# Expert layers: counting matmuls and the write of the gates moved into the next step

## The chip, the cores and the metric

One core of one Trainium2 chip runs the whole program. The metric is the time of one execution on the device, in microseconds. The engines are TensorE (PE; its weight loads are PEld), VectorE (DVE), ScalarE (ACT), GpSimd (POOL) and SyncE (SP), which issues the transfers.

## What is computed

The input x has 16 sequences of 512 tokens with 128 features. A mixture of experts, an attention with 16 heads, and the same mixture of experts again are each added to x. The change is in the expert layer, which runs twice:

```python
C = int(Tt * K / Ee * CAPACITY_FACTOR) + 1
logits = jnp.einsum('btd,ed->bte', x, Wr)
top_vals, top_idx = jax.lax.top_k(logits, K)
w = jax.nn.softmax(top_vals, axis=-1)
flat_e = top_idx.reshape(Bb, Tt * K)
oh = jax.nn.one_hot(flat_e, Ee, dtype=jnp.int32)
pos_all = jnp.cumsum(oh, axis=1) - oh
pos = jnp.take_along_axis(pos_all, flat_e[..., None], axis=-1)[..., 0]
keep = pos < C
...
expert_out = jnp.einsum('becd,edf->becf', expert_in, We)
...
out = jnp.einsum('btk,btkd->btd', w, gathered)

x = x + 0.5 * _L0_ffn_ref(_layernorm(x, axis=-1), L0_ffn_Wr, L0_ffn_We)
x = x + _L0_attn_ref(_layernorm(x, axis=-1), ...)
x = x + 0.5 * _L0_ffn_ref(_layernorm(x, axis=-1), L0_ffn_Wr, L0_ffn_We)
```

There are 8 experts, each token picks 2, and an expert takes only its first 193 picks of a sequence.

## The kernel before

x lies on chip the whole time, as 16 sequences of 4 tiles of 128 tokens. The expert layer computes all 8 experts for every token and weighs the products with gates, which are zero for experts that were not picked or were full. One step of the layer works on sequence b, while the routing of b + 1 and the statistics of b + 2 run between. Each engine has its own program; they wait for one another's semaphores, and each engine runs its instructions in the order written. The step is a function per engine (`step`, lines 313 to 330 for TensorE, 569 to 595 for VectorE).

TensorE, per step: it transposes the normalised sequence b + 1 (`turn_h`, L277), multiplies the first tile of b with four experts (`experts_lo`, the low product, L303) and with the other four (`experts_hi`, the high product, L310), multiplies b + 1 with the router (`logits`, L286), does the low and high products of tiles 1 to 3, and at the end counts, for every token of b + 1, the earlier picks of each expert (`places`, four bf16 matmuls, L293 and L295). Logits and counts lie in the two halves of one PSUM bank; the logits of b + 1 wait until all twelve parts of b's routing are done, the write of b's gates among them, the counts for the picks (7 parts).

VectorE, per step: statistics of b + 2 (L476, four instructions), then for each tile four additions to x of gate times low product (L561): two of this tile, two of the tile before. Between the additions stand the aggregates of the statistics (L483), eps (L490), the shift (L495, which waits for POOL's root L419), and the nine pieces of the routing of b + 1 (`route`): 0 the copy of the logits (L509), 1 the two largest, 2 their indices and gap, 3 the compares (L526, L528), 4 the picks (L532), 5 to 7 the weights (L536 to L545, with an exponential of ScalarE), and 8 the gates (L553): weight times (count below 193). `ROUTE_AFTER` says behind which addition (tile, number) a piece stands; piece 8 is last, behind the last addition of the step.

ScalarE copies the transposes, scales the four high products of a tile with the gates (L374) and normalises b + 2. POOL sums the scaled products (L426, L433), adds them to x (L440), and takes the root.

In either layer steps (counted from 0, like the sequences) run as straight code at the ends and as a loop of two steps in the middle (first layer: steps 1 to 8; second layer: 1 to 12). Steps 9 to 15 of the first layer have pieces of the attention between the tiles, and the second layer's first sequence is prepared inside the end of the attention (`late`). The last two steps of a layer have no statistics, the last no routing.

Of the kernel before, what the change touches and what calls it, by code (L numbers as in the profile page):

```python
# [57 lines left out]
def after(b, n):  # L58


    return not isinstance(b, int) or b > n
# [96 lines left out]
def expert_layer(nc, ctx, tag, x, consts, weights, banks, guard, x_in=None, out=None):  # L158
# [67 lines left out]
    def added(b, t, e):  # L226


        n = b * T + t
        if isinstance(n, int) and n == 0 and e < 2:  # L230
            return e + 1
        if isinstance(n, int) and n == NSEQ * T - 1 and e >= 2:
            return n * HE + e + 1
        return n * HE + (-1, 1, 4, 6)[e]
# [35 lines left out]
    def tensor_part():  # L270
        def turn_h(b, par):
            guard.turn_h(b)
            pe.wait_ge(hn_done, b + 1)
            if after(b, 0):
                pe.wait_ge(hT_copied, b)
            for t in range(T):
                mm = nc.tensor.transpose(hT_ps[:, t * P:(t + 1) * P], hn[:, t, :], consts.ident)  # L277
            mm.then_inc(hT_out, 1)

        def logits(b, par):  # L280
            guard.logits(b)
            pe.wait_ge(hT_copied, b + 1)
            if after(b, 0):
                pe.wait_ge(route_step, b * RT)
            for t in range(T):
                mm = nc.tensor.matmul(route_ps[:, 0, t, :], hT[par][:, t * P:(t + 1) * P], wrT[:],  # L286
                                      start=True, stop=True)
            mm.then_inc(logits_out, 1)

        def places(b):  # L290

            pe.wait_ge(route_step, b * RT + PICKED)
            nc.tensor.matmul(route_ps[:, 1, :, :], consts.before_b, picks[:], start=True, stop=False)  # L293
            for s in range(1, T):
                mm = nc.tensor.matmul(route_ps[:, 1, s:T, :], consts.ones_b, picks[:, 0:T - s, :],  # L295
                                      start=False, stop=(s == T - 1))
            mm.then_inc(places_out, 1)

        def experts_lo(b, par, t):
            guard.experts_lo(b, t)  # L300
            if after(b, 0):
                pe.wait_ge(acc_step, added(b - 1, t, HE - 1))
            nc.tensor.matmul(lo_ps[t][:], hT[par][:, t * P:(t + 1) * P], we[:, 0:HE, :],  # L303
                             start=True, stop=True).then_inc(lo_out, 1)

        def experts_hi(b, par, t):
            guard.experts_hi(b, t)
            if after(b, 0) or t >= 2:
                pe.wait_ge(scaled_done, b * T + t - 1)
            nc.tensor.matmul(hi_ps[t % 2][:], hT[par][:, t * P:(t + 1) * P], we[:, HE:E, :],  # L310
                             start=True, stop=True).then_inc(hi_out, 1)

        def step(b, par, half, this, next1, next2, between=None):
            if next1:
                turn_h(b + 1, 1 - par)
            if this:
                experts_lo(b, par, 0)
                if between:
                    between(0)
                experts_hi(b, par, 0)  # L320
            if next1:
                logits(b + 1, 1 - par)
            if this:
                for t in range(1, T):
                    if between:
                        between(t)
                    experts_lo(b, par, t)
                    experts_hi(b, par, t)
            if next1:
                places(b + 1)  # L330

        def begin():
            pe.wait_ge(consts.placed, consts.N_PLACED)
            pe.wait_ge(weights.placed, weights.N_PLACED)

        def late(what):
            if what == "turn_h":
                turn_h(0, 0)
            elif what == "logits":
                logits(0, 0)  # L340
            elif what == "places":
                places(0)

        return Part(begin, step, None, late)

    def scalar_part():
# [121 lines left out]
    def vector_part():  # L468
        def statistics(b, par, half):
            if x_in is not None:  # L470
                dve.wait_ge(x_loaded[par], half * DMA + DMA)
            guard.statistics(b)
            if after(b, 0):
                dve.wait_ge(nmr_done, b)
            for t in range(T):
                ins = nc.vector.bn_stats(bn[:, t, :], xt(b, t))  # L476
            ins.then_inc(bn_done, 1)

        def aggregate(b):
            dve.wait_ge(bn_done, b + 1)  # L480
            dve.sem_inc(dve_passed, 1)
            for t in range(T):
                ins = nc.vector.bn_aggr(mean_var[:, t, :], bn[:, t, :])  # L483
            ins.then_inc(stats_done, 1)

        def add_eps(b):
            dve.wait_ge(stats_done, b + 1)
            if after(b, 0):
                dve.wait_ge(rstd_done, b)
            nc.vector.tensor_scalar(veps[:], mean_var[:, :, 1], EPS, 0.0, ALU.add, ALU.add).then_inc(eps_added, 1)  # L490

        def shift_mean(b):

            dve.wait_ge(rstd_done, b + 1)
            nc.vector.scalar_tensor_tensor(out=nmr[:], in0=mean_var[:, :, 0], scalar=-1.0, in1=rstd[:],  # L495
                                           op0=ALU.mult, op1=ALU.mult).then_inc(nmr_done, 1)
# [60 lines left out]
        def add_expert(b, par, t, e):  # L557

            if e > 0:
                dve.wait_ge(acc_step, added(b, t, e - 1))  # L560
            nc.vector.scalar_tensor_tensor(out=xt(b, t), in0=lo_ps[t][:, e, :],  # L561
                                           scalar=gates[par][:, t, e:e + 1], in1=xt(b, t),
                                           op0=ALU.mult, op1=ALU.add).then_inc(acc_step, 1)


        ROUTE_AFTER = {(1, 0): [0], (1, 1): [1], (1, 2): [2], (1, 3): [3], (2, 0): [4], (2, 2): [5],
                       (2, 3): [6], (3, 0): [7], (3, 3): [8]}

        def step(b, par, half, this, next1, next2, between=None):
            if next2:  # L570
                statistics(b + 2, par, half)
            for t in range(T):
                if between:
                    between(t)
                if this:
                    dve.wait_ge(lo_out, b * T + t + 1)
                    if t == 0:
                        dve.wait_ge(route_step, b * RT + RT)
                        dve.wait_ge(hn_done, b + 1)
                for k in range(HE):  # L580
                    if this and k % 2 == 0:
                        add_expert(b, par, t, k // 2)
                    elif this and t > 0:
                        add_expert(b, par, t - 1, 2 + k // 2)
                    elif this and after(b, 0):
                        add_expert(b - 1, 1 - par, T - 1, 2 + k // 2)
                    if next1:
                        for n in ROUTE_AFTER.get((t, k), []):
                            route(b + 1, 1 - par, n)
                    if next2 and (t, k) == (0, 0):  # L590
                        aggregate(b + 2)
                    if next2 and (t, k) == (0, 1):
                        add_eps(b + 2)
                    if next2 and (t, k) == (1, 0):
                        shift_mean(b + 2)
# [23 lines left out]
        def late(what):  # L619
            if what in ("statistics0", "statistics1"):  # L620
                b = int(what[-1])
                statistics(b, b, 0)
                aggregate(b)
                add_eps(b)
            elif what in ("normalise0", "normalise1"):
                shift_mean(int(what[-1]))
                normalise(int(what[-1]))
            elif what == "turn_h":
                dve.wait_ge(hT_out, 1)
                nc.vector.tensor_copy(hT[0][:], hT_ps[:]).then_inc(hT_copied, 1)  # L630
            elif what == "logits":
                for n in range(3):
                    route(0, 0, n)
            elif what == "places":
                for n in (3, 4):
                    route(0, 0, n)
            elif what == "gates":
                for n in range(5, 9):
                    route(0, 0, n)

        return Part(begin, step, end, late)
# [824 lines left out]
```

## Time and profile before

| | |
|---|---|
| median of 3 runs | 845.43 us (840.67 to 852.52) |
| profiled execution, its own time | 841.81 us |
| span of its trace | 840.1 us |
| busy: TensorE, VectorE, ScalarE, POOL | 792.5 (94%), 753.3 (90%), 630.4 (75%), 538.3 (64%) us |
| granted TensorE clock, mean | 0.977 of full speed |

The profile is of one execution. Times in it count from the span's start. Busy shares are averages over three stages: the first expert layer ends at about 167 us, the attention at about 700, and the rest is the second expert layer. Ends of matmuls are modelled and overlap, so the distance from one matmul's start to the next one's tells more than its length. The view in order of time gives for each instruction its start, its length, engine, line, tiles, and in brackets how long its engine was idle ahead of it and what ended that; neighbours of the same kind are merged (x4).

### The profile page before, as it was taken

Reading aid. Unit: us, or ns where it says so; the run is one execution under the profiler, and the core shown is the slowest. Engines: PE = TensorE matmul, PEld = TensorE weight load, DVE = VectorE, ACT = ScalarE, POOL = GpSimd, SP = SyncE. Lnnn points to the kernel's source line nnn. Section 1 sums busy time; section 2 is a strip of 40 time slices with the busy share of each in tenths; the row PEclk is TensorE's granted clock in tenths of the full one; section 3 lists DMA queues with packets and bytes.
Section 4 is the critical chain, followed back from the end, with each engine's and each line's share of the span. In section 5 each row is a group of like instructions: output and inputs, shape, how many; then the busy total and the mean of one; then the engine's idle time right before and its main releaser. Section 6 shows DMA issues by size and latency. Waiting matters only on the chain.

```text
span 840.1 us, 23658 instructions
## 1 busy us (share of the span) xinstructions
PE 792.5 (94%) x6498; PEld 383.7 (46%) x6498; DVE 753.3 (90%) x2543; ACT 630.4 (75%) x1529; POOL 538.3 (64%) x838
## 2 busy tenths in 40 slices
PE   3999989889999999999999999999999999999997
PEld 2445444334344444444544444454444434545543
DVE  4999989898999999999999999999999637999996
ACT  3777777615887888888888888888878756777775
POOL 3778878853575575576566566567463435887887
PEclk9999999967999999999999999999999989999999
DMA  6600000331332332332332232233231000010011
GB/s 172 129 0 0 0 1 20 125 125 66 107 113 96 100 117 91 106 111 87 112 111 98 96 113 96 93 113 112 96 102 39 2 1 14 26 36 26 25 38 38
DMA packets 54969, 62.02 MB, mean 74 GB/s; under 512 B 5696, under 2 KB 48576, under 8 KB 54784
## 3 DMA queue, kind: packets, MB, share of 16 engines
q1 hardware_dynamic: 54912, 61.33, 22.9%
q8 instruction: 27, 0.44, 0.2%
q14 instruction: 30, 0.25, 0.1%
HBM read 31.70 MB, written 29.36 MB: 73 GB/s over the span
## 4 chain that ended last, share of the span: by engine, by line
PE 35%; DVE 20%; issue 13%; POOL 10%; DVEq 2%; ACT 1%; POOLq 1%
DVE att_neg_max L1196 12%; PE bank L1002 11%; PE bank L962 7%; PE bank L985 4%; PE bank L303 3%; DVE x L561 2%; PE bank L310 2%; PE bank L1035 2%; POOL att_probs L1156 2%; POOL att_rest L889 2%; POOL att_rstd L1168 2%; PE bank L1041 2%; POOL moe_rstd L419 1%; ACT att_probs L1075 1%; PE bank L1017 1%
## 5 line engine op out<-in xcount | busy, mean ns | idle before, releaser
L1196 DVE TENSOR_REDUCE att_neg_max<-bank 128x1 bf16<-128x512 f32 (+3 forms) x704 | 405.6, 635 | 17.0 <-PE bank L965 13.6
L1075 ACT ACTIVATE att_probs<-bank 128x512 f32<-128x512 f32 x640 | 346.5, 594 | 71.8 <-PE bank L985 70.8
L1156 POOL TENSOR_SCALAR_AFFINE_SELECT att_probs<-att_probs 128x512 f32<-128x512 f32 x256 | 158.7, 635 | 211.7 <-ACT att_probs L1075 211.6
L985 PE MATMUL bank<-att_q_st,att_k_st 53*128 53x512 bf16 (+3 forms) x1024 | 216.8, 303 | 2.5 <-ACT att_probs L1075 2.5
L962 PE MATMUL bank<-att_k_st,att_q_st 51*128 51x384 bf16 (+2 forms) x768 | 183.6, 282 | 13.4 <-DVE att_neg_max L1196 7.4
L374 ACT ACTIVATE moe_scaled<-bank,moe_gates 128x128 f32<-128x128 f32 x512 | 145.2, 370 | 63.3 <-PE bank L310 57.3
L1002 PE MATMUL bank<-att_probs,att_v 128*32 128x512 f32 (+3 forms) x2048 | 178.7, 444 | 1.2 <-POOL att_probs L1156 1.2
L561 DVE SCALAR_TENSOR_TENSOR x<-bank,moe_gates,x 128x128 f32 (+1 forms) x512 | 160.1, 338 | 14.4 <-PE bank L303 13.5
L962 PEld LDWEIGHTS bank<-att_k_st,att_q_st 51*128 51x128 bf16 x768 | 71.3, 95 | 190.1 <-DVE att_neg_max L1196 144.5
L965 PE MATMUL bank<-att_k_st,att_q_st 64*128 64x128 bf16 x1024 | 157.4, 222 | 0.1
L303 PE MATMUL bank<-moe_we,moe_hT 128*128 128x512 f32 x256 | 134.2, 606 | 0.8 <-DVE x L1239 0.8
L310 PE MATMUL bank<-moe_we,moe_hT 128*128 128x512 f32 x256 | 131.8, 597 | 0.5 <-ACT moe_scaled L374 0.5
L426 POOL TENSOR_TENSOR moe_part<-moe_scaled 128x256 f32<-128x256 f32 x128 | 93.9, 734 | 43.1 <-ACT moe_scaled L374 41.2
L965 PEld LDWEIGHTS bank<-att_k_st,att_q_st 64*128 64x128 bf16 x1024 | 85.2, 96 | 0.7 <-DVE att_neg_max L1196 0.2
L310 PEld LDWEIGHTS bank<-moe_we,moe_hT 128*128 128x128 f32 x256 | 48.8, 191 | 62.4 <-issue 57.1
L985 PEld LDWEIGHTS bank<-att_q_st,att_k_st 53*128 53x128 bf16 x1024 | 68.6, 94 | 13.1 <-ACT att_probs L1075 7.1
L1002 PEld LDWEIGHTS bank<-att_probs,att_v 128*32 128x32 f32 x2048 | 47.7, 108 | 49.3 <-issue 31.7
L440 POOL TENSOR_TENSOR x<-x,moe_part 128x128 f32 (+1 forms) x128 | 59.4, 464 | 13.0 <-DVE x L561 12.9
L303 PEld LDWEIGHTS bank<-moe_we,moe_hT 128*128 128x128 f32 x256 | 43.9, 192 | 31.6 <-issue 22.2
L433 POOL TENSOR_TENSOR moe_part<-moe_part 128x128 f32<-128x128 f32 x128 | 58.1, 454 | 0.2
L352 ACT ACTIVATE moe_hn<-x,moe_nmr,moe_rstd 128x128 f32 (+1 forms) x120 | 49.4, 494 | 8.4 <-DVE moe_nmr L495 8.4
L419 POOL TENSOR_TENSOR moe_rstd<-moe_veps,f_consts 128x4 f32<-128x4 f32 x32 | 32.5, 1017 | 20.8 <-DVE moe_veps L490 19.6
(83 smaller groups left out, 868.4 us busy)
## 6 DMA issues: line engine op xcount, KB each, us to landing
qk_parts<-att_parts SPq DMA_DIRECT2D x32, 384.0 KB, 2.5
att_q_st<-qk_parts SPq DMA_DIRECT2D x64, 192.0 KB
att_k_st<-qk_parts SPq DMA_DIRECT2D x64, 192.0 KB
qk_parts<-att_parts SPq DMA_DIRECT2D x32, 256.0 KB, 2.1
x<-in_L_attn_x SPq DMA_DIRECT2D x16, 256.0 KB, 2.8
qk_parts<-att_parts SPq DMA_DIRECT2D x32, 128.0 KB, 1.7
out<-x SPq DMA_DIRECT2D x16, 256.0 KB, 2.3
moe_we<-in_L_ffn_We SPq DMA_DIRECT2D x1, 512.0 KB, 5.2
```

Source lines behind the costliest of these rows:

```text
L303: nc.tensor.matmul(lo_ps[t][:], hT[par][:, t * P:(t + 1) * P], we[:, 0:HE, :], start=True, stop=True).then_inc(lo_out, 1)
L310: nc.tensor.matmul(hi_ps[t % 2][:], hT[par][:, t * P:(t + 1) * P], we[:, HE:E, :], start=True, stop=True).then_inc(hi_out, 1)
L374: ins = nc.scalar.activation(scaled[t % 2][:, e, :], hi_ps[t % 2][:, e, :], ACT.Copy, scale=gates[par][:, t, HE + e:HE + e + 1])
L426: nc.gpsimd.tensor_tensor(part2[t % 2][:], scaled[t % 2][:, 0:2, :], scaled[t % 2][:, 2:4, :], ALU.add).then_inc(part_step, 1)
L561: nc.vector.scalar_tensor_tensor(out=xt(b, t), in0=lo_ps[t][:, e, :], scalar=gates[par][:, t, e:e + 1], in1=xt(b, t), op0=ALU.mult, op1=AL ...
L962: nc.tensor.matmul(max_ps[m % RING][:, at:at + width - P], q_st[par][low:low + FAR_ROW, r, i * P:(i + 1) * P], k_st[par][low:low + FAR_ROW ...
L965: mm = nc.tensor.matmul(max_ps[m % RING][:, at + width - P:at + width], q_st[par][low:low + SIDE, r, i * P:(i + 1) * P], k_st[par][low:low ...
L985: mm = nc.tensor.matmul(exp_ps[m % RING][:, c:c + S - j * P], k_st[par][low:low + FINE_ROW, r, j * P:(j + 1) * P], q_st[par][low:low + FIN ...
L1002: mm = nc.tensor.matmul(pv_ps[VW * hh:VW * (hh + 1), j * P:S], v[par][:, j, 4 * half_at + hh, ab, :], probs[g % 2][:, n, c:c + S - j * P], ...
L1075: nc.scalar.activation(probs[g % 2][:, n, :], exp_ps[m % RING][:], ACT.Exp).then_inc(exp_done, 1)
L1156: nc.gpsimd.affine_select(out=view, in_=view, compare_op=ALU.is_ge, fill=0.0, base=0, pattern=[[0, 4], [1, P]], channel_multiplier=-1).the ...
L1196: nc.vector.tensor_reduce(neg_max[par][:, g // 2, 1 - g % 2, heads[0]:heads[0] + len(heads), i], max_ps[m % RING][:, 0:len(heads) * width] ...
```

## The change

On TensorE the counting matmuls of a sequence leave the end of the step before and stand in the sequence's own step, behind the transposes of the next sequence and ahead of the first low product. On VectorE piece 8 leaves the end of the step before and stands in the sequence's own step behind the statistics, ahead of the first addition. For the second layer's first sequence both leave the end of the attention and stand in the layer's first step. Nothing else is changed.

```diff
--- before.py
+++ after.py
@@ -314,6 +314,7 @@
             if next1:
                 turn_h(b + 1, 1 - par)
             if this:
+                places(b)
                 experts_lo(b, par, 0)
                 if between:
                     between(0)
@@ -326,8 +327,6 @@
                         between(t)
                     experts_lo(b, par, t)
                     experts_hi(b, par, t)
-            if next1:
-                places(b + 1)
 
         def begin():
             pe.wait_ge(consts.placed, consts.N_PLACED)
@@ -338,8 +337,6 @@
                 turn_h(0, 0)
             elif what == "logits":
                 logits(0, 0)
-            elif what == "places":
-                places(0)
 
         return Part(begin, step, None, late)
 
@@ -564,7 +561,7 @@
 
 
         ROUTE_AFTER = {(1, 0): [0], (1, 1): [1], (1, 2): [2], (1, 3): [3], (2, 0): [4], (2, 2): [5],
-                       (2, 3): [6], (3, 0): [7], (3, 3): [8]}
+                       (2, 3): [6], (3, 0): [7]}
 
         def step(b, par, half, this, next1, next2, between=None):
             if next2:
@@ -573,6 +570,8 @@
                 if between:
                     between(t)
                 if this:
+                    if t == 0:
+                        route(b, par, 8)
                     dve.wait_ge(lo_out, b * T + t + 1)
                     if t == 0:
                         dve.wait_ge(route_step, b * RT + RT)
@@ -635,7 +634,7 @@
                 for n in (3, 4):
                     route(0, 0, n)
             elif what == "gates":
-                for n in range(5, 9):
+                for n in range(5, 8):
                     route(0, 0, n)
 
         return Part(begin, step, end, late)
```

## Rows read from the trace of the kernel before

**Rows 1.** Busy time by stretch, second layer's loop; last: granted clock, DMA share, GB/s.

```profile
714.62:803.12 88.50, 86.61 (x320) 43.89 (x320) 84.57 (x492) 65.42 (x220) 72.62 (x130) 1.00 0.10 30
```

**Rows 2.** VectorE in order of time: start, us, engine, line, tiles; two loop steps.

```profile
740.96 0.17 DVE L553 SCALAR_TENSOR_TENSOR moe_gates<-bank,moe_gw 128x32 f32<-128x32 f32 x1
...
741.40 0.87 DVE L476 BATCH_NORM_STATS2 moe_bn<-x 128x6 f32 x4 [0.27 <-issue]
...
743.93 0.18 DVE L509 COPY moe_L<-bank 128x32 f32<-128x32 f32 x1
...
744.45 0.68 DVE L495 SCALAR_TENSOR_TENSOR moe_nmr<-moe_mean_var,moe_rstd 128x4 f32<-128x4 f32 x1 [0.34 <-POOL moe_rstd L419]
...
745.05 0.34 DVE L561 SCALAR_TENSOR_TENSOR x<-bank,moe_gates,x 128x128 f32 x1
...
750.05 0.17 DVE L553 SCALAR_TENSOR_TENSOR moe_gates<-bank,moe_gw 128x32 f32<-128x32 f32 x1
...
750.15 0.85 DVE L476 BATCH_NORM_STATS2 moe_bn<-x 128x6 f32 x4
...
750.92 0.33 DVE L561 SCALAR_TENSOR_TENSOR x<-bank,moe_gates,x 128x128 f32 x1
...
752.72 0.18 DVE L509 COPY moe_L<-bank 128x32 f32<-128x32 f32 x1
...
758.65 0.17 DVE L553 SCALAR_TENSOR_TENSOR moe_gates<-bank,moe_gw 128x32 f32<-128x32 f32 x1
```

**Rows 3.** TensorE in order of time, the same two loop steps.

```profile
746.51 1.02 PE L310 MATMUL bank<-moe_we,moe_hT 128*128 128x512 f32 x2
...
747.66 0.19 PE L293 MATMUL bank<-moe_picks,bf_consts 128*128 128x32 bf16 x1
...
748.33 1.02 PE L303 MATMUL bank<-moe_we,moe_hT 128*128 128x512 f32 x2
...
749.19 1.02 PE L310 MATMUL bank<-moe_we,moe_hT 128*128 128x512 f32 x2
...
750.28 1.06 PE L286 MATMUL bank<-moe_wrT,moe_hT 128*128 128x8 f32 x8
```

**Rows 4.** VectorE in order of time, second layer's step 14, without statistics.

```profile
820.34 0.17 DVE L553 SCALAR_TENSOR_TENSOR moe_gates<-bank,moe_gw 128x32 f32<-128x32 f32 x1
...
822.68 0.35 DVE L561 SCALAR_TENSOR_TENSOR x<-bank,moe_gates,x 128x128 f32<-128x128 f32 x1 [0.96 <-PE bank L303]
...
822.95 0.18 DVE L509 COPY moe_L<-bank 128x32 f32<-128x32 f32 x1
...
828.42 0.17 DVE L553 SCALAR_TENSOR_TENSOR moe_gates<-bank,moe_gw 128x32 f32<-128x32 f32 x1
```

**Rows 5.** POOL in order of time, in the loop's same stretch.

```profile
744.39 0.72 POOL L426 TENSOR_TENSOR moe_part<-moe_scaled 128x256 f32<-128x256 f32 x1
```

**Rows 6.** All engines in order of time, first layer's step 0.

```profile
22.63 0.18 DVE L509 COPY moe_L<-bank 128x32 f32<-128x32 f32 x1
...
24.43 0.73 POOL L426 TENSOR_TENSOR moe_part<-moe_scaled 128x256 f32<-128x256 f32 x1 [1.46 <-ACT moe_scaled L374]
...
24.58 0.63 DVE L526 TENSOR_TENSOR moe_first<-f_consts,moe_top_at 128x32 f32<-128x32 f32 x1
...
28.55 0.18 DVE L553 SCALAR_TENSOR_TENSOR moe_gates<-bank,moe_gw 128x32 f32<-128x32 f32 x1
```

**Rows 7.** VectorE in order of time: first layer's step 11, second layer's step 1.

```profile
123.36 0.18 DVE L509 COPY moe_L<-bank 128x32 f32<-128x32 f32 x1
...
129.30 0.17 DVE L553 SCALAR_TENSOR_TENSOR moe_gates<-bank,moe_gw 128x32 f32<-128x32 f32 x1
...
708.31 0.18 DVE L509 COPY moe_L<-bank 128x32 f32<-128x32 f32 x1
...
714.62 0.17 DVE L553 SCALAR_TENSOR_TENSOR moe_gates<-bank,moe_gw 128x32 f32<-128x32 f32 x1
```

**Rows 8.** VectorE in order of time, the first layer's step 10.

```profile
116.78 0.17 DVE L536 TENSOR_SCALAR moe_den<-moe_egap 128x4 f32<-128x4 f32 x1 [0.93 <-ACT moe_egap L364]
```

## The prediction

> **What bounds the kernel now.** I read the busy times by stretch first. In the second layer's loop (ten steps) TensorE is busy 86.61 us of 88.50 and VectorE 84.57 [rows 1]. Neither engine has room, so a step is set by the hand-overs between them, and the order of work in time has to be read. VectorE's rows, from one write of the gates to the next, give steps of 750.05 - 740.96 = 9.09 and 758.65 - 750.05 = 8.60 us, in turn [rows 2]. I cut each step in two at the copy of the logits (L509), which sits right behind the first add that needs the second low product. Head, gates to copy: 2.97 and 2.67. Tail, copy to the next gates: 6.12 and 5.93. The pair is 17.69 us. The first layer's loop has the same two kinds of step in turn, and I price it by this pair.
>
> The longer head carries the loop's jump: gates to statistics is 0.44 us there and 0.10 in the other, 0.34 more [rows 2]. TensorE's side of the same pair [rows 3]: one product goes 0.86 us after another (748.33 to 749.19), so the fourth high product, begun at 746.51, is over at 747.37, and the count of places begins at 747.66: a wait of 0.29 for the picks. The high product of 749.19 is over at 750.05 and the logits begin at 750.28: 0.23, the write of the gates (0.17) and its signal. These two waits are what the change can take from TensorE: 0.52 us of a pair of 17.69.
>
> **The change, part by part.** Nothing is added or removed: the same four counting matmuls and the same write of the gates run, later. No transfer is issued by either, and no queue of SP or POOL is passed.
>
> *TensorE's half.* The count of places (0.20 of PE time, begun at 747.66 ahead of transposes and the product at 748.33) now stands behind the transposes. The picks are then long there, so the 0.29 wait goes. Behind the count come the first low and high product, then the logits, which still wait for the gates: that wait takes the time up. So this half is worth nothing unless the gates come early too.
>
> *VectorE's half.* They come later. The statistics now stand ahead of the gates: from their start to that of the next instruction is 750.92 - 750.15 = 0.77 us [rows 2]. Queued on TensorE behind the logits' wait is the second low product, and behind that VectorE's first add of the second tile. What this hand-over costs when no statistics lie between can be read directly: two steps, step 14 of each layer (steps count from 0), have none, and there the gates go at 820.34, VectorE waits 0.96 us for the low product, and the copy comes at 822.95: a head of 2.61, not of 0.77 less [rows 4]. The first layer's twin has 2.61 as well. The head is thus a path through TensorE that does not shrink when the statistics leave it. The new step is statistics 0.77 + head 2.61 + tail, and 0.34 for the jump in every second one.
>
> *The tail.* It could shrink, as VectorE would reach it 0.36 (2.97 - 2.61) earlier against TensorE in one step and 0.06 in the other. In the tail of today stands a wait for POOL's root (0.34 at 744.45) and a multiply of 128x4 that takes 0.68 us, ending with POOL's sum of 744.39 + 0.72; from the copy (743.93) to the add behind it (745.05) is 1.12 us [rows 2, 5]. If the root is early and POOL still, all of that but some 0.27 (822.68 to 822.95, one instruction's pace [rows 4]) could go: a tail of 6.12 - 0.85 = 5.27. Against that: where VectorE reaches the tail straight from the wait for the low product, as it will in every step now, it meets POOL further on. In the first layer's step 0 the compare of 24.58 takes 0.63, ending within 0.05 us of POOL's sum (24.43 + 0.73), and the tail is 28.55 - 22.63 = 5.92 [rows 6]. Its step 11, of the same kind, has 129.30 - 123.36 = 5.94 [rows 7]. Step 14 of the second layer, without the multiply, has 5.47 [rows 4], and 5.64 with an unhindered one (0.17, as long as the gates' own write). The second layer's step 1 has 714.62 - 708.31 = 6.31 [rows 7]: it meets the late root and the blocked multiply as well. I take 5.9, about the mean of the four (5.95), as these rows are in the new order's phase; the bounds are 5.27 and 6.31.
>
> The Trainium skill (SBUF — State Buffer, "Who interferes with whom") says that a VectorE instruction with two SBUF inputs and a GpSimd instruction that reads SBUF exclude each other for their whole length, and the first one in goes on. The row of the compare agrees: both its inputs lie in SBUF, and it ends with POOL's row. By that rule the blocking moves along the step and does not vanish, and the tail stays near 5.9; without it the tail would be near 5.3.
>
> *The sum over the loops.* New pair: 2 x (0.77 + 2.61 + 5.9) + 0.34 = 18.90, against 17.69: 1.21 more. Pairs: six in the second layer (steps 2 to 13), four in the first (steps 1 to 8): 12.1 us. TensorE does not bound this: its pair less the waits is at most 17.69 - 0.52 = 17.17.
>
> *Outside the loops.* Steps 9 to 13 of the first layer have attention pieces between the tiles. Bounds are 0 (a piece fills the wait for the low product) and 0.77 (all of the statistics). Step 10 is nearest to the upper: VectorE waits 0.93 there for the exponential of the gap [rows 8], and ScalarE, which makes it, comes behind the logits. I take 0.77 for it and 0.2 for each of the others, 1.5. Step 0 of each layer and step 1 of the second have a late TensorE and no price here, at most 3 x 0.77 = 2.3. The last two steps of a layer have no statistics: nothing.
>
> Sum: 12.1 + 1.5 = 13.6 us. The profiled execution took 841.81 (span 840.1), so 855.4. The median of the runs is 845.43, that is 3.6 above the profiled one, and on it the sum gives 859.0. I give 856, nearer to the execution whose rows I used.
>
> **Rivals.**
>
> *VectorE is relieved as well (small loss).* The wait for the root goes, POOL is not met again, and tails are 5.3. Pair: 2 x (0.77 + 2.61 + 5.3) + 0.34 = 17.70, no change in the loops; with 1.5 outside, 843 on the profiled time, 847 on the median. For it: the root is asked for right behind the gates' first adds and gets the 0.36 us of extra lead. Against it: the four tails above.
>
> *The collisions grow (slower by over 2%).* The place is the tail, the price is the longest one seen, 6.31, in every step: pair 2 x (0.77 + 2.61 + 6.31) + 0.34 = 19.72, 2.03 more, 20.3 over ten pairs; with 1.5 outside, 863.6, or 867.2 on the median. It decides from a mean tail of some 6.06 on, where ten pairs cost 15.3 and the whole is 2% of 841.81 (16.8). For it: a blocked multiply and blocked compares can fall in one step. Against: in the step with 6.31 the compares were free, and in the steps with 5.92 and 5.94 the multiply was; what is held up in one place reaches the next when POOL has passed.
>
> *TensorE is the bound (faster).* If TensorE alone set the steps, the two waits of 0.52 a pair would be gain: 5.2 us, 836.6. For it: 98% busy. Against: TensorE would have to find the gates ready, and they are written 0.77 later, behind work of the same VectorE that is 96% busy. It would need VectorE to have idle time in front of the gates for the statistics.
>
> By the same rule of the Trainium skill as above the first of these rivals is the one that fails, and its 843 would become the 855 of the forecast.
>
> **How the numbers follow.** Forecast (tails 5.6 to 6.05, 849 to 858.5 on the profiled time): 0.60. Relieved: 0.19. Collisions grow: 0.17. TensorE the bound: 0.04. The predicted time is the forecast's 856. The range has to hold 8 in 10: the forecast, most of the relieved case on the median, and the lower part of the collisions, 846 to 863. A change of 2% is about what a measurement of this kernel can tell from none (the runs before go from 840.67 to 852.52). Slower by over 2% is 859 on the profiled time and 862 on the median: the collisions' case, 0.17. Faster by over 2% (825) is beyond even the third rival: 0.01. The rest, 0.82, is within 2%.
>
> **What would show it.** Right: VectorE's gates behind the statistics, and in every loop step a wait of VectorE for the low product (L303) some 0.5 us long where there is none now; head 2.61 in both kinds of step; steps of about 9.3 and 9.6; TensorE's wait for the gates in front of the logits (L286) grown from 0.23 to some 0.4 to 0.8, its wait for the picks gone; multiply L495 and compares L526, L528 that end with POOL's rows. Wrong: steps of 8.85 or under (tail near 5.3, or the logits not waiting), a head well off 2.61, a TensorE clock below its full level in the loops (it is 1.00 there now [rows 1]), or a time that changes in the attention part, which nothing here touches.

## The result

| | before | after |
|---|---|---|
| median of 20 runs each | 841.58 us (838.85 to 852.52) | 855.58 us (849.97 to 864.40) |
| profiled execution, own time | 841.81 us | 854.82 us |
| span of its trace | 840.1 us | 853.1 us |
| granted TensorE clock, mean | 0.977 | 0.974 |

The ratio of after to before is 1.0144, with a 95% interval of 1.0119 to 1.017: slower, by less than 2%. It is taken over the fast runs, those within 1.5% of the fastest of their kernel; the two medians, over all runs, stand at 1.0166. The forecast was 856 us, with 846 to 863 as its range. Line numbers of the expert layer in the kernel after are smaller by three on VectorE, ScalarE and POOL: gates L550, copy L506, statistics L473, additions L558, shift L492, compares L523 and L525, ScalarE's scaling L371, POOL L416 to L437; TensorE's are the same as before.

**The clock makes the spread.** TensorE's granted clock falls to 0.50 (1.2 GHz) as the first expert layer gives way to the attention, and again near the attention's end. In the ten us from 170 on, around or ahead of the fall at the attention's start, TensorE was busy for 7.62 and 7.18 only. In after's trace it falls twice more, for some 3.5 us each, inside the first layer (from 126 and from 150 on), where before's trace has 1.00 throughout. How much of an execution lies at the lower level differs: the mean clock of after's 20 runs goes from 0.959 to 0.98. Over them the span falls by some 5.8 us for each 0.01 of mean clock, and a straight line through them gives 853.3 at a clock of 0.975; before's is at 841.7 (7 runs). At equal clock the two kernels are thus 11.6 us apart. I give the span at 0.975 for each experiment too, from the line through its own executions, since a median of four can lie in a low stretch of clock.

Busy time by stretch, kernel before (us; PE, PEld, DVE, ACT, POOL, each with its count; then clock, DMA share, GB/s):

```profile
170.00:180.00 10.00, 7.62 (x41) 2.95 (x40) 9.52 (x25) 1.37 (x2) 8.18 (x9) 0.71 0.38 128
180.00:190.00 10.00, 9.87 (x51) 4.87 (x49) 9.17 (x19) 1.91 (x5) 1.03 (x2) 0.50 0.38 133
...
680.00:690.00 10.00, 10.00 (x63) 4.53 (x55) 2.25 (x7) 4.56 (x9) 2.27 (x4) 0.69 0.01 2
```

The same view, kernel after; the last line is the second layer's loop, which answers to [rows 1]:

```profile
126.00:130.00 4.00, 3.83 (x8) 1.78 (x9) 1.42 (x11) 0.60 (x1) 2.30 (x4) 0.59 0.00 0
...
170.00:180.00 10.00, 7.18 (x39) 3.06 (x38) 8.24 (x23) 4.73 (x15) 9.71 (x16) 1.00 0.26 97
...
190.00:200.00 10.00, 9.75 (x49) 4.88 (x49) 9.16 (x18) 1.91 (x5) 0.00 (x0) 0.50 0.37 140
...
680.00:690.00 10.00, 8.92 (x58) 2.31 (x51) 1.91 (x12) 6.34 (x14) 2.50 (x4) 0.67 0.00 0
...
714.00:810.00 96.00, 88.43 (x326) 45.00 (x325) 87.36 (x499) 66.32 (x223) 75.00 (x134) 1.00 0.10 28
```

In the loop the clock is full on both sides, so the loss there is none of the clock's. TensorE was busy for 98% of that stretch and is now for 92%, VectorE for 91% after 96%: both lose, as they do when each waits for the other.

**Two loop steps of after.** VectorE in order of time; these lines answer to [rows 2]:

```profile
740.34 0.17 DVE L550 SCALAR_TENSOR_TENSOR moe_gates<-bank,moe_gw 128x32 f32<-128x32 f32 x1
...
742.74 0.35 DVE L558 SCALAR_TENSOR_TENSOR x<-bank,moe_gates,x 128x128 f32 x1 [0.62 <-PE bank L303]
743.00 0.18 DVE L506 COPY moe_L<-bank 128x32 f32<-128x32 f32 x1
743.10 0.32 DVE L492 SCALAR_TENSOR_TENSOR moe_nmr<-moe_mean_var,moe_rstd 128x4 f32<-128x4 f32 x1
...
745.48 0.49 DVE L525 TENSOR_TENSOR moe_second<-f_consts,moe_top_at 128x32 f32<-128x32 f32 x1
...
746.16 0.24 DVE L529 TENSOR_TENSOR moe_picks<-moe_first,moe_second 128x32 bf16<-128x32 f32 x1
...
747.70 0.51 DVE L542 TENSOR_TENSOR moe_gw<-moe_g,moe_w 128x32 f32<-128x32 f32 x1
...
749.13 0.87 DVE L473 BATCH_NORM_STATS2 moe_bn<-x 128x6 f32 x4 [0.15 <-issue]
749.92 0.17 DVE L550 SCALAR_TENSOR_TENSOR moe_gates<-bank,moe_gw 128x32 f32<-128x32 f32 x1
...
752.31 0.35 DVE L558 SCALAR_TENSOR_TENSOR x<-bank,moe_gates,x 128x128 f32 x1 [0.56 <-PE bank L303]
752.58 0.18 DVE L506 COPY moe_L<-bank 128x32 f32<-128x32 f32 x1
752.68 0.46 DVE L492 SCALAR_TENSOR_TENSOR moe_nmr<-moe_mean_var,moe_rstd 128x4 f32<-128x4 f32 x1
...
754.41 0.71 DVE L519 TENSOR_TENSOR moe_gap<-moe_top 128x4 f32<-128x4 f32 x1
...
758.52 0.86 DVE L473 BATCH_NORM_STATS2 moe_bn<-x 128x6 f32 x4
759.30 0.17 DVE L550 SCALAR_TENSOR_TENSOR moe_gates<-bank,moe_gw 128x32 f32<-128x32 f32 x1
```

The reader sees the gates behind the statistics, and in each step a wait for the low product that was not there before. Steps are 749.92 - 740.34 = 9.58 and 9.38 us, the pair 18.96 (17.69 before). Head, gates to copy: 2.66 in both. Tail, copy to the next statistics: 6.13 with the loop's jump, 5.94 without. Statistics to gates: 0.79 and 0.78.

TensorE in order of time, the same steps, which answer to [rows 3]:

```profile
740.56 1.06 PE L286 MATMUL bank<-moe_wrT,moe_hT 128*128 128x8 f32 x8 [0.72 <-DVE moe_gates L550]
...
746.71 0.60 PE L277 MATMUL bank<-f_consts,moe_hn 128*128 128x128 f32 x4
747.15 0.18 PE L293 MATMUL bank<-moe_picks,bf_consts 128*128 128x32 bf16 x1
...
750.15 1.06 PE L286 MATMUL bank<-moe_wrT,moe_hT 128*128 128x8 f32 x8 [0.93 <-DVE moe_gates L550]
```

The count follows the transposes with no wait for the picks. The wait in front of the logits has grown from 0.23 to 0.72 and 0.93.

POOL in order of time, one sum in each step and the addition to x behind the first:

```profile
745.47 0.46 POOL L437 TENSOR_TENSOR x<-x,moe_part 128x128 f32 x1
...
754.36 0.73 POOL L423 TENSOR_TENSOR moe_part<-moe_scaled 128x256 f32<-128x256 f32 x1 [0.41 <-ACT moe_scaled L371]
```

The subtraction that makes the gap (754.41, L519) ends at 755.12, POOL's sum at 755.09; the compare of 745.48 ends at 745.97, POOL's addition at 745.93. The Trainium skill (SBUF — State Buffer, "Who interferes with whom") has an exclusive lock between a VectorE instruction with two inputs in SBUF and a GpSimd instruction that reads SBUF. Both pairs are of that kind, and these ends agree with it.

**Where the 13.0 us lie.** Writes of the gates in order of time, kernel before: sequences 9, 14 and 15 of the first layer (the others are in [rows 2, 4, 6 and 7]):

```profile
99.86 0.17 DVE L553 SCALAR_TENSOR_TENSOR moe_gates<-bank,moe_gw 128x32 f32<-128x32 f32 x1
...
151.66 0.17 DVE L553 SCALAR_TENSOR_TENSOR moe_gates<-bank,moe_gw 128x32 f32<-128x32 f32 x1
160.59 0.17 DVE L553 SCALAR_TENSOR_TENSOR moe_gates<-bank,moe_gw 128x32 f32<-128x32 f32 x1
```

Kernel after: sequences 1, 9, 14 and 15 of the first layer, 2, 14 and 15 of the second:

```profile
29.55 0.17 DVE L550 SCALAR_TENSOR_TENSOR moe_gates<-bank,moe_gw 128x32 f32<-128x32 f32 x1
...
104.13 0.16 DVE L550 SCALAR_TENSOR_TENSOR moe_gates<-bank,moe_gw 128x32 f32<-128x32 f32 x1
...
157.89 0.17 DVE L550 SCALAR_TENSOR_TENSOR moe_gates<-bank,moe_gw 128x32 f32<-128x32 f32 x1
167.42 0.17 DVE L550 SCALAR_TENSOR_TENSOR moe_gates<-bank,moe_gw 128x32 f32<-128x32 f32 x1
...
721.39 0.17 DVE L550 SCALAR_TENSOR_TENSOR moe_gates<-bank,moe_gw 128x32 f32<-128x32 f32 x1
...
833.35 0.17 DVE L550 SCALAR_TENSOR_TENSOR moe_gates<-bank,moe_gw 128x32 f32<-128x32 f32 x1
841.44 0.17 DVE L550 SCALAR_TENSOR_TENSOR moe_gates<-bank,moe_gw 128x32 f32<-128x32 f32 x1
```

A step of after begins with its statistics, 0.77 ahead of its gates; a step without statistics begins with the gates. With that, from step to step:

| stretch | forecast | measured | how |
|---|---|---|---|
| layer 1, start and step 0 | no price | +0.2 | 29.55 - 0.77 - 28.55 |
| layer 1, steps 1 to 8 | +4.8 | +3.3 | (104.13 - 29.55) - (99.86 - 28.55) |
| layer 1, steps 9 to 14 | +1.5 | +3.3 | + 0.77 + (157.89 - 104.13) - (151.66 - 99.86), and + 0.6 for step 14 (9.53 against 8.93) |
| attention, layer 2's steps 0 and 1 | 0 | -0.8 | (721.39 - 0.77 - 167.42) - (714.62 - 160.59) |
| layer 2, steps 2 to 13 | +7.3 | +7.0 | + 0.77 + (833.35 - 721.39) - (820.34 - 714.62) |
| layer 2, step 14 | 0 | 0.0 | 8.09 against 8.08 |
| sum | 13.6 | 13.0 | 841.44 - 828.42 |

The 3.3 of steps 9 to 14 hold the two falls of the clock, which the part on the forecast takes up.

### The profile page after: what moved, and what is told of

It reads as the page before. It is cut to its first block and busy times, and to the rows that moved or that the text cites. A ratio compares the mean times of both kernels' runs of the same rounds, so it can differ in the third digit from the quotient of the medians.

```text
span 853.1 us, 23668 instructions
## 1 busy us (share of the span) xinstructions
PE 795.0 (93%) x6498; PEld 386.0 (45%) x6498; DVE 754.2 (88%) x2543; ACT 630.8 (74%) x1529; POOL 539.0 (63%) x838
## 5 line engine op out<-in xcount | busy, mean ns | idle before, releaser
L371 ACT ACTIVATE moe_scaled<-bank,moe_gates 128x128 f32<-128x128 f32 x512 | 145.9, 372 | 88.3 <-PE bank L310 50.8
L558 DVE SCALAR_TENSOR_TENSOR x<-bank,moe_gates,x 128x128 f32 (+1 forms) x512 | 161.4, 339 | 32.5 <-PE bank L303 28.4
L303 PE MATMUL bank<-moe_we,moe_hT 128*128 128x512 f32 x256 | 138.5, 623 | 0.8 <-DVE x L1238 0.8
L310 PE MATMUL bank<-moe_we,moe_hT 128*128 128x512 f32 x256 | 133.6, 604 | 0.5 <-ACT moe_scaled L371 0.5
L437 POOL TENSOR_TENSOR x<-x,moe_part 128x128 f32 (+1 forms) x128 | 59.2, 463 | 6.6 <-DVE x L558 6.4
L303 PEld LDWEIGHTS bank<-moe_we,moe_hT 128*128 128x128 f32 x256 | 44.4, 193 | 32.7 <-issue 26.4
L286 PE MATMUL bank<-moe_wrT,moe_hT 128*128 128x8 f32 x256 | 34.3, 260 | 20.1 <-DVE moe_gates L550 19.3
```

The lines of the kernel that those rows point to most:

```text
L371: ins = nc.scalar.activation(scaled[t % 2][:, e, :], hi_ps[t % 2][:, e, :], ACT.Copy, scale=gates[par][:, t, HE + e:HE + e + 1])
```

## The experiments

The theory is that of the forecast: the price is VectorE's half alone, since the 0.77 of statistics now stand ahead of a hand-over (gates, logits, low product, VectorE's first addition of the second tile) that keeps its length, and the tail does not shrink because POOL is met in it wherever VectorE comes from. The rivals: that TensorE's half costs or gains something, that TensorE sets the steps, and that the head is not a path but VectorE's own work.

### The gates back in front of the statistics

Against after, on VectorE:

```diff
@@ step
+            if this:
+                route(b, par, 8)
             if next2:
...
-                    if t == 0:
-                        route(b, par, 8)
```

> Both parts stay moved into the next step, but VectorE writes the gates ahead of the statistics. If the price of the change is that the statistics lie ahead of the gates, it goes: gates to copy takes 2.6 to 3.0 us with the statistics inside it, copy to the next gates about 6, a pair of steps 17.4 to 17.8 instead of 18.96, the time 838 to 844 us. If the price is the counting matmuls' new place behind the transposes (they delay the first low product), or the move of the gates across the step's end as such, it stays at 852 to 858.

Median 843.59 us of 4 runs, ratio to before 1.0002 (0.9943 to 1.006); 841.9 at a clock of 0.975. VectorE in order of time, second layer's loop:

```profile
753.11 0.17 DVE L550 SCALAR_TENSOR_TENSOR moe_gates<-bank,moe_gw 128x32 f32<-128x32 f32 x1
...
755.77 0.18 DVE L506 COPY moe_L<-bank 128x32 f32<-128x32 f32 x1
...
762.01 0.19 DVE L550 SCALAR_TENSOR_TENSOR moe_gates<-bank,moe_gw 128x32 f32<-128x32 f32 x1 [0.23 <-ACT moe_scaled L371]
```

The whole loss is gone, though both pieces of work still stand in the later step. The head is 2.66 here too (2.73 in the other step), now with the statistics inside it: they are covered again. Steps are 8.90 and 9.00, and the pair of 17.90 is 0.2 above before's. The trace names ScalarE for the 0.23 of idle time ahead of the gates, but by the program the scaling that the gates have to wait for is over a step earlier. The idle time stands in every second step, where before had 0.27 of the loop's jump [rows 2], and the kernel with both remedies has the same 0.23 with no releaser named; I take it for the jump. So where the gates stand as against the step's border matters little, and that they stand behind the statistics is the loss.

### Each half of the change alone

The counting matmuls moved and the gates where they were; the second layer's first sequence is counted where it was, too. Against after:

```diff
-                places(b)
+                if not (tag == "moe2" and isinstance(b, int) and b == 0):
+                    places(b)
...
-                       (2, 3): [6], (3, 0): [7]}
+                       (2, 3): [6], (3, 0): [7], (3, 3): [8]}
...
-                    if t == 0:
-                        route(b, par, 8)
...
```

> Only TensorE's half: the counting matmuls stand behind the next step's transposes, the gates stay at the end of VectorE's step, behind its last addition (the second layer's first sequence is counted in the old place). If TensorE's half is worth nothing, since the wait for the gates ahead of the logits takes up what the wait for the picks gives back: 838 to 844 us, the same as before, and the wait for the gates about 0.3 us longer in the steps that waited for the picks. If TensorE set the steps: 834 to 837. If the counting matmuls' new place is what costs: 850 or more.

Median 843.62 us of 4 runs, ratio 1.0007 (0.9935 to 1.0079); 840.8 at a clock of 0.975. Steps 9.09 and 8.60, as in [rows 2]. TensorE in order of time:

```profile
756.07 0.18 PE L293 MATMUL bank<-moe_picks,bf_consts 128*128 128x32 bf16 x1
...
758.57 1.06 PE L286 MATMUL bank<-moe_wrT,moe_hT 128*128 128x8 f32 x8 [0.44 <-DVE moe_gates L553]
```

The wait for the picks (0.29 in [rows 3]) is gone and the wait for the gates takes it up, 0.44: TensorE's half is worth nothing, as forecast.

The gates moved and the counting matmuls where they were. Against after:

```diff
-                places(b)
...
+            if next1:
+                places(b + 1)
...
```

> Only VectorE's half: the counting matmuls stay at the end of TensorE's step, the gates stand behind the statistics. If the statistics ahead of the gates are the whole price: 852 to 858 us, a pair of steps near 18.96, a wait of VectorE for the second low product of about 0.6 us in every step. If the two halves share it: 845 to 850.

Median 861.01 us of 4 runs, ratio 1.0207 (1.0149 to 1.0264). All four executions had a low mean clock (0.964 to 0.969); the line through them gives 854.3 at 0.975, beside after's 853.3. The trace decides: steps of 9.57 and 9.38, as in after, and VectorE's waits from 720 to 810 us (total, times, longest), nearly after's own (5.7, 10, 0.6):

```profile
DVE x L561 <- PE bank L303: 5.8, 10, 0.6
```

VectorE's half alone makes the loops' part of the change.

### Is the head a path through TensorE?

Against after, on TensorE, ahead of the call of the logits:

```diff
+            early_lo = this and not between
+            if early_lo:
+                experts_lo(b, par, 1)
...
-                    experts_lo(b, par, t)
+                    if t > 1 or not early_lo:
+                        experts_lo(b, par, t)
```

In steps without attention pieces the second tile's low product goes ahead of the logits, so VectorE's first addition of that tile no longer hangs on the gates.

> The changed kernel, but in steps without attention pieces TensorE does the second tile's low product ahead of the logits, so that VectorE's first addition of the second tile no longer hangs behind the gates. If the head (gates, logits, low product, addition) is the path: VectorE's wait of 0.6 us for that product goes, gates to copy falls from 2.66 to about 2.05, and the time by up to 20 x 0.6 = 12 us, to 843 to 849. If the step is held by something else behind the gates (ScalarE's exponential, POOL's sums), what the head gives is waited for in the tail, and it stays at 852 to 858.

Median 849.55 us of 4 runs, ratio 1.0083 (1.002 to 1.0147). Its four executions had clocks of 0.965 to 0.973; the line through them gives 843.1 at 0.975, and after's slope of 5.8 us for each 0.01 gives 845.3, so I take 843 to 845. The wait for L303 is gone and the head falls from 2.66 to 1.95 and 2.02, 1.35 a pair. The tails, copy to statistics, grow from 6.13 and 5.94 to 6.39 and 6.13; the pair is 18.05, 0.91 less. VectorE in order of time:

```profile
755.94 0.18 DVE L510 COPY moe_L<-bank 128x32 f32<-128x32 f32 x1
...
756.47 0.68 DVE L496 SCALAR_TENSOR_TENSOR moe_nmr<-moe_mean_var,moe_rstd 128x4 f32<-128x4 f32 x1 [0.35 <-POOL moe_rstd L420]
```

The head is the path. But VectorE, early again, finds POOL's root late and then the blocked multiply, as in [rows 2]: a third of the gain goes back.

### What POOL holds up in the tail

POOL's three additions of a tile are cut to 8 of the 128 columns, the other columns of its sum are left out; one kernel cuts them in after, the other in before:

```diff
-            nc.gpsimd.tensor_tensor(part2[t % 2][:], scaled[t % 2][:, 0:2, :], scaled[t % 2][:, 2:4, :],
+            nc.gpsimd.tensor_tensor(part2[t % 2][:, :, 0:8], scaled[t % 2][:, 0:2, 0:8], scaled[t % 2][:, 2:4, 0:8],
...
-            nc.gpsimd.tensor_tensor(xt(b, t), xt(b, t), part1[t % 2][:], ALU.add).then_inc(part_step, 1)
+            nc.gpsimd.tensor_tensor(x8(b, t), x8(b, t), part1[t % 2][:, 0:8], ALU.add).then_inc(part_step, 1)
```

POOL's rows shrink from 0.73 us for the first sum to a mean of 0.26, and from 0.46 for the other two to 0.20 and 0.21.

> The changed kernel with POOL's three additions per tile on 8 of 128 columns (sums, part and x); most of the high products are thus not added to x, nothing else is left out. If the tail of about 5.9 us is held up by POOL's additions: the compares, the weight and the gap's subtraction take their short lengths (0.18 and less), the tail falls to 5.0 to 5.4, a pair of steps to 17.2 to 17.9, the time to 838 to 845 us. If the tail is VectorE's own pace: 852 to 858.

> The kernel before with the same short additions on POOL (8 of 128 columns; most of the high products are not added to x). If POOL's additions hold VectorE up there too, some 0.5 to 1.0 us a step fall away and TensorE becomes the bound (pair near 17.0): 832 to 838 us, so that it stays faster than the changed kernel with the same cut by the part of the head that TensorE sets, 4 to 10 us. If POOL has no part in it: 838 to 844.

On after: median 833.36 us of 10 runs, ratio to before 0.991 (0.9874 to 0.9945), 833.0 at a clock of 0.975, which is below what either theory expected. VectorE in order of time:

```profile
754.56 0.18 DVE L509 COPY moe_L<-bank 128x32 f32<-128x32 f32 x1
...
757.92 0.17 DVE L536 TENSOR_SCALAR moe_den<-moe_egap 128x4 f32<-128x4 f32 x1 [0.36 <-ACT moe_egap L364]
...
759.66 0.86 DVE L476 BATCH_NORM_STATS2 moe_bn<-x 128x6 f32 x4
```

The head stays at 2.66, the tail is 759.66 - 754.56 = 5.10 (5.32 in the other step): 0.8 less than after's, even though VectorE now waits 0.36 for ScalarE's exponential. So the 5.9 of the forecast was POOL's doing, and a kernel in which POOL were out of the way would have had the "relieved" rival's tail and less. The pair of steps, 17.32, is what the first theory expected; the rest of the gain lies outside the loops (step 14 of the first layer took 7.46, and 9.53 in after).

On before: median 824.77 us of 4 runs, ratio 0.9821 (0.9753 to 0.989), 824.9 at a clock of 0.975, below both expectations; the steps of the second layer's loop are 8.32 to 8.35, the tail is 5.09. Busy time by stretch (columns as above):

```profile
720.00:810.00 90.00, 90.00 (x344) 47.38 (x343) 80.00 (x522) 69.76 (x237) 35.78 (x142) 1.00 0.11 32
```

TensorE is busy all the time: now it is the bound, at 8.34 a step. That is 16.68 a pair, under the 17.17 which I had given as the most that TensorE needs. Between the two cut kernels lie 8.6 us of medians: the change costs less where TensorE already limits the kernel before.

### Taking one blocked instruction away

In before, the shift's multiply goes from VectorE to POOL, behind the root:

```diff
+            nc.gpsimd.tensor_tensor(mean2[:], mean_var[:, :, 0], mean_var[:, :, 0], ALU.add).then_inc(mean_step, 1)
...
+            nc.gpsimd.tensor_tensor(neg_mean[:], mean2[:], consts.half_neg, ALU.mult).then_inc(mean_step, 1)
...
+            nc.gpsimd.tensor_tensor(nmr[:], neg_mean[:], rstd[:], ALU.mult).then_inc(nmr_done, 1)
...
-            dve.wait_ge(rstd_done, b + 1)
-            nc.vector.scalar_tensor_tensor(out=nmr[:], in0=mean_var[:, :, 0], scalar=-1.0, in1=rstd[:],
-                                           op0=ALU.mult, op1=ALU.mult).then_inc(nmr_done, 1)
```

> The kernel before with the expert layers' shift (minus mean times the root, 128x4) taken from VectorE to POOL, as three small operations behind the root. If the wait for the root and the held-up multiply in VectorE's tail are time of the path: the tails fall from 6.12 and 5.93 to some 5.3 to 5.6, TensorE's waits for picks and gates shrink, a pair comes to 16.9 to 17.3, the time to 834 to 839 us. If what is taken away here is met at POOL's next additions instead: 839 to 845.

Median 844.1 us of 10 runs, ratio 1.0009 (0.997 to 1.0047); 840.6 at a clock of 0.975. VectorE in order of time, second layer's loop:

```profile
751.26 0.49 DVE L527 TENSOR_TENSOR moe_gap<-moe_top 128x4 f32<-128x4 f32 x1
...
752.12 0.49 DVE L533 TENSOR_TENSOR moe_second<-f_consts,moe_top_at 128x32 f32<-128x32 f32 x1
```

The multiply of 0.68 and its wait of 0.34 are out of VectorE's program, and the tails remain 6.11 and 5.92. VectorE comes earlier to the gap and the compares, and POOL's sum (751.01, 0.72) and addition (752.10, 0.46) hold them there. This agrees with the forecast's "what is held up in one place reaches the next", but it does not show it by itself: the three small operations stand between POOL's root and its sum and put that sum off by 0.7 us (from 750.30 to 751.01), so that POOL comes later too.

### Both remedies together

The gates in front of the statistics and the second low product ahead of the logits, the two edits above in one kernel.

> Both parts moved, the gates ahead of the statistics, and TensorE does the second low product ahead of the logits in steps without attention pieces. If with the statistics behind the gates the head is filled by VectorE's own work (2.67 us), the product's earlier place gives nothing: 838 to 845 us. If the product is still waited for: 832 to 837.

Median 840.98 us of 10 runs, ratio 0.9971 (0.9942 to 0.9999); 839.2 at a clock of 0.975. Steps 8.84 each, a pair of 17.68 against 17.69 before (17.90 with the gates alone put back): in the loops it equals the kernel before, as the first of the two cases expected. The interval ends just under 1, within 2% all the same; I don't call it a better kernel.

## Why the prediction was right

The mechanism of the loops was right, and the runs show it. That the traces differ by 13.0 us where 13.6 was forecast is partly luck, as the terms show. The choice of the profiled execution as the base (841.81) and not of the median of three (845.43) was right: the median of 20 runs before is 841.58.

- **The step as a sum.** Statistics 0.77, head 2.61, tail 5.9, jump 0.34: 18.90 a pair, measured 18.96. The head came out at 2.66, the tail at 5.94, the wait for L303 at 0.56 and 0.62 (some 0.5 was forecast). The step without statistics [rows 4] was the right place to read the head from: it showed the hand-over bare. The two experiments on its ends show why. With the statistics inside the head it keeps its 2.66; with TensorE's product moved out it shrinks.
- **The jump was over-sized.** 0.34 was forecast, and the two tails differ by 6.13 - 5.94 = 0.19. The statistics show 0.15 of idle time behind it. The head's 2 x 0.05 made up for most of it in the pair.
- **TensorE's half is worth nothing.** Right, as its run alone shows. TensorE's waits for the gates were forecast at 0.4 to 0.8 and are 0.72 and 0.93, 1.65 a pair. That size was already in my own numbers: 18.90 less TensorE's 17.17 leaves 1.73.
- **The tail at 5.9 is POOL's.** Right: cut POOL short and it is 5.1. The blocked instructions are only in part those that I named. The multiply came down from 0.68 to 0.32 and 0.46; the compares are held up in one step of the pair, the gap in the other (0.71); the weights' last product takes 0.51, but it was held up before the change too (0.46 at 757.49).
- **The loops of the first layer, mis-sized.** 4.8 forecast, 3.3 measured. The common pair there is 9.37 + 9.69, 1.2 above before's 17.86, so the price is right; but two of the eight steps fell out of the pattern (8.97 and 8.64, at 77.13 and 95.49). The second layer has one (8.87, at 778.26), and that one shows what happens.

VectorE of after in order of time, that step:

```profile
783.40 0.18 DVE L525 TENSOR_TENSOR moe_second<-f_consts,moe_top_at 128x32 f32<-128x32 f32 x1
...
783.76 0.18 DVE L529 TENSOR_TENSOR moe_picks<-moe_first,moe_second 128x32 bf16<-128x32 f32 x1
...
785.24 0.17 DVE L542 TENSOR_TENSOR moe_gw<-moe_g,moe_w 128x32 f32<-128x32 f32 x1
```

POOL of after, the same step:

```profile
783.38 0.52 POOL L437 TENSOR_TENSOR x<-x,moe_part 128x128 f32 x1
```

Here the compare took 0.18, where at 745.48 it took 0.49, and POOL's addition took 0.52 and not 0.46: I read this as a near tie in which VectorE went first and POOL gave way. The picks take 0.06 less and the last product 0.34 less; with the 0.31 of the compare that is 0.71, all of what the step is shorter (9.58 to 8.87). The other two show the same in the compare (0.18) and in POOL's addition (0.52). Three of the ten steps of this kind fell so; had all ten, the pair would be 8.87 + 9.38 = 18.25, an estimate: 0.71 of the 1.20 us between the forecast's pair and that of the "relieved" rival hangs on this tie.

- **Outside the loops, off by the clock.** 1.5 forecast for steps 9 to 13, 2.7 there and 0.6 in step 14. Step 10 cost 0.77 as forecast (10.19 against 9.42), step 9 0.37. Steps 11 and 12, priced at 0.2 each, cost 0.92 and 1.04 (11.55 against 10.63, 12.78 against 11.74), but that is not the statistics' price. Of the two falls of after's clock inside the layer the first lies in step 11 (126 to 130 us): two products that follow on each other at 0.86 us elsewhere take 1.64 and 1.70 there (begun at 126.66 and 128.30), VectorE waits 0.82 longer for the low product, and step 12 begins with TensorE late: VectorE waits 0.60 for the first low product (136.41), where before has no such wait. In the runs with the gates alone moved and with the low product first, whose VectorE has after's order and whose clock is full in these two steps, they take 10.62 and 11.76, and 10.61 and 12.04: next to nothing in three of the four. The second lies in step 13 (150 to 154 us), and step 14 then has TensorE go from product to logits without a wait: it is late there by itself (+0.6).

VectorE in order of time, step 11, kernel before and kernel after:

```profile
123.09 0.35 DVE L561 SCALAR_TENSOR_TENSOR x<-bank,moe_gates,x 128x128 f32<-128x128 f32 x1 [1.61 <-PE bank L303]
```

```profile
128.54 0.35 DVE L558 SCALAR_TENSOR_TENSOR x<-bank,moe_gates,x 128x128 f32<-128x128 f32 x1 [2.43 <-PE bank L303]
```

TensorE was busy for 2.48 of the 4 us ahead of the first fall and for 1.75 of the 4 us ahead of the second. Whether the change brings these falls about is open: each of the eight other kernels' traces has one or two between 114 and 154 us, those with the gates in their old place too, and before's has none.

- **The attention.** It was to stay as it was, and with the second layer's first two steps it is 0.8 shorter. The spells of low clock lie in that part; the same part takes 553.2 us in after and 560.0 in the run with the gates alone moved, so a difference of 0.8 says nothing.

The two differences nearly cancel (-1.5 and +1.8), and so do the jump and the head. The total is therefore nearer (13.0 against 13.6) than its terms, and part of the 13.0 is the clock's: at equal clock the difference is 11.6. The nearer thing to a test is the pair, 18.96 against 18.90.

**The rivals.** "Relieved" would have needed tails of 5.3 in every step. With POOL cut short they are there, and after itself has 5.51, 5.20 and 5.42 in the three steps in which VectorE won the tie; in the other seventeen POOL's collisions are met. "Collisions grow" needed a mean of 6.06; after's tails were 6.04 on the mean, jump included, so 5.94 without it. "TensorE the bound" is refuted by its growing wait for the gates, and only the kernel with POOL cut and the gates at their old place is bound that way.

## What to carry to other kernels

Work that stands behind a write on which another engine waits can be covered by the hand-over; moved in front of the write it cost its whole length here, 0.77 us a step, although nothing was added. To price such a move, look for a step of the same trace that lacks the moved work: it shows the hand-over's own length, and so whether it will shrink. A wait saved in front of one engine's instruction (here 0.29 us, for the picks) was worth nothing, since a later instruction waited for the same partner.

## What was new about the hardware

- What POOL costs VectorE in a step hung on how long POOL's rows are more than on which of VectorE's instructions met them. Shortening POOL's rows was worth 22.2 us on after and 17.5 us on before (855.58 to 833.36, 842.3 to 824.77; the wait for the root is part of that), which is more than the change itself, while moving the one instruction on which most of the time showed from VectorE to POOL was worth nothing.
- Who goes first in a near tie was worth 0.71 us of a step, and the same code fell either way from step to step (9.58 and 8.87).
- Executions of one kernel differ by 14 us (849.97 to 864.40), in step with their mean granted clock (0.98 to 0.96). In the traces, one for each kernel, the 1.2 GHz level is found at the start of the attention, near its end and in spells of some 3.5 to 7 us in the first layer; near the end, the run with the low product first is at 0.50 from 680 to 700, the one with both remedies at 1.00. Between kernels that differ by 1%, the mean granted clock belongs beside each time.
